# Block kernel (gated scan mixer, then routed experts): where TensorE waits as it enters the output and down projections

## The chip, the cores and the metric

The kernel runs on one core of one Trainium2 chip. The metric is the device time of one execution in microseconds. The kernel before took 505.88 us (median of three runs, 505.38 to 506.28).

## The reference

The input is 8 sequences of 1024 tokens with 256 features, in float32. What matters here:

```python
def mixer(x):                        # x normalised over its 256 features
    xp, z = split(x @ w_in)          # 512 channels each
    xc = silu(causal_conv(xp, 4 taps) + conv_b)
    h = h * 0.9 + 0.1 * (xc_t @ w_B) # 16 states, along the sequence
    return ((h @ w_C) * silu(z)) @ w_out
def experts(x):                      # x normalised again
    idx = top_k(x[:, 0, :] @ Wr + br, 2)      # by the first token of a sequence
    return mean over the 2 experts of gelu(x @ W1 + b1) @ W2 + b2
x = x + mixer(norm(x))
x = x + experts(norm(x))
```

## The kernel before

The 8192 tokens are cut into 16 chunks of 512. The work is a pipeline over chunks: step s runs the mixer's first part of chunk a = s, the output projection of chunk o = s - 1 and the experts of chunk f = s - 2. Each engine has its own program (`block.tensor`, `block.vector` and so on), written out by hand in order, and the programs meet at semaphores only. The first steps are an opening written out singly, steps 4 to 13 are a loop, and the last ones are written out again.

Every float32 product is made of three: an operand is split into a high and a low part, and TensorE computes high x high, high x low and low x high into the same accumulator. Two shapes of matmul fill its time. `project` (line 1290) makes 512-column products into a bank `blk` (six for a bank: first high and low weights with the high activations for both halves k, then the high weights with the low activations), and `state_in` (line 1466) makes eight 512-column ones into `turn`. `tokens` (line 1413) makes 256-column products into `tok`: here the activations are loaded as weights (`LDWEIGHTS`, 128 columns) and the weight matrix moves. One call of `tokens` makes two groups of three, lines 1419, 1420 and 1421. `out_proj` (line 1453) calls it four times for each of two halves h, 48 products in a row. `down` (line 1440) does the same, 24 products for h = 0 and 12 of h = 1, then comes `state_out` (line 1478, four 512-column products), then the other 12.

In `step` of TensorE (line 1571) the order is: the four `xp` projections, `out_proj` of both halves, the four `z` projections, the four `up` projections, `state_in`, `down` with `state_out` inside. So 256-column stretches start behind `xp` (the last `project`) or behind `state_in`, and in the last two steps behind `up`. At these 30 places `behind` (line 1424) stands ahead of the first product. It increments `paced`, a semaphore that nobody waits for, waits for a tail semaphore and increments `paced` three times more (`PACE`). The tail is incremented by the fourth-last matmul ahead: line 1297 in `project` (`x_tail`, `up_tail`) and line 1474 in `state_in` (`state_tail`). TensorE's instructions are handed out in order, so a wait holds all that stands behind it; a matmul call issues its weight load and its matmul.

Of the kernel before, what the change touches and what calls it, by code (L numbers as in the profile page):

```python
# [16 lines left out]
SQ = 32  # L17
QUADS = P // SQ
EARLY = 2
PACE = 3  # L20


def build_block(nc, x, w_in, conv_w, conv_b, w_B, w_C, w_out, Wr, br, W1, b1, W2, b2, out):
# [9 lines left out]
    KD = D // P  # L33
    JD = DI // P
    JF = TOP_K * KD
# [7 lines left out]
    with ExitStack() as ctx:  # L43
# [48 lines left out]
        w_out_hi, w_out_lo = sb("w_out_hi", [P, JD, D], F32R), sb("w_out_lo", [P, JD, D], F32R)  # L92
        w2_hi, w2_lo = sb("w2_hi", [P, TOP_K, KD * D], F32R), sb("w2_lo", [P, TOP_K, KD * D], F32R)
# [6 lines left out]
        y_hi, y_lo = sb("y_hi", [P, JD, CH], F32R), sb("y_lo", [P, JD, CH], F32R)  # L100
# [76 lines left out]
        paced = sem("paced")  # L177
# [1059 lines left out]
        def _(pe):  # L1237
            mm = nc.tensor.matmul
# [48 lines left out]
                    nc.tensor.transpose(blk[0][:, k * P:(k + 1) * P], by_token(normed2, 0)[:, k * P:(k + 1) * P],  # L1287
                                        ident[:]).then_inc(token_turned, 1)

            def project(bank, whi, wlo, his, los, ready, c, sem_out, fourth_last=None, between=None):  # L1290

                dst = bank[:]
                for k in range(KD):
                    if ready is not None:
                        pe.wait_ge(ready[0], c * KD + k + 1)
                    ins = mm(dst, whi(k), his(k), start=(k == 0), stop=False)  # L1296
                    if k == KD - 1 and fourth_last is not None:
                        ins.then_inc(fourth_last, 1)
                    mm(dst, wlo(k), his(k), start=False, stop=False)  # L1299
                    if k == 0 and between is not None:  # L1300
                        between()
                for k in range(KD):
                    if ready is not None:
                        pe.wait_ge(ready[1], c * KD + k + 1)
                    ins = mm(dst, whi(k), los(k), start=False, stop=(k == KD - 1))  # L1305
                ins.then_inc(sem_out, 1)

            def in_proj(a, j, part, bank, sem_out, between=None):
# [101 lines left out]
                            lambda k: w1_lo[:, 1, k * D + m * P:k * D + (m + 1) * P],  # L1410
                            lambda k: his[:, k, :], lambda k: los[:, k, :], None, 0, up_ready)

            def tokens(h, j, last, his, los, whi, wlo):


                for n in range(2):
                    rows = slice((2 * h + n) * P, (2 * h + n + 1) * P)
                    dst = tok[h][:, n * D:(n + 1) * D]
                    mm(dst, his[:, j, rows], whi, start=(j == 0 and n == 0), stop=False, skip_group_check=True)  # L1419
                    mm(dst, his[:, j, rows], wlo, start=False, stop=False, skip_group_check=True)  # L1420
                    ins = mm(dst, los[:, j, rows], whi, start=False, stop=(last and n == 1), skip_group_check=True)  # L1421
                return ins

            def behind(tail, count):
                pe.sem_inc(paced, 1)
                pe.wait_ge(tail, count)
                for _ in range(PACE):
                    pe.sem_inc(paced, 1)

            def down_tile(f, n, dst, js=range(JF)):  # L1430
                rows = slice(n * P, (n + 1) * P)
# [8 lines left out]
            def down(f, h, js=range(JF), tail=None):  # L1440
                for j in js:
                    if h == 0:
                        pe.wait_ge(g_lo, f * JF + j + 1)
                        if isinstance(f, int) and f == LAST - 1 and j % KD == 0:
                            pe.wait_ge(w2_lo_set, LAST // 2 * TOP_K + j // KD + 1)
                    if j == 0 and tail is not None:
                        behind(*tail)
                    t, cols = j // KD, slice(j % KD * D, (j % KD + 1) * D)
                    ins = tokens(h, j, j == JF - 1, hid_hi, hid_lo, w2_hi[:, t, cols], w2_lo[:, t, cols])
                if js[-1] == JF - 1:  # L1450
                    ins.then_inc(down_ready, 1)

            def out_proj(o, h, tail=None):
                pe.wait_ge(done, o * 2 + h + 1)
                for j in range(JD):
                    if h == 0:
                        if isinstance(o, int) and o == LAST and j:
                            pe.wait_ge(last_y_lo, j)
                        else:
                            pe.wait_ge(y_lo_set, o * JD + j + 1)  # L1460
                    if j == 0 and tail is not None:
                        behind(*tail)
                    ins = tokens(h, j, j == JD - 1, y_hi, y_lo, w_out_hi[:, j, :], w_out_lo[:, j, :])
                ins.then_inc(mixed, 1)

            def state_in(a):
                bank = u_bank(a)
                for j in range(JD):
                    pe.wait_ge(xc_hi_set, a * JD + j + 1)
                    mm(bank[:], b_mix[:, j, :], xc_hi[:, j, :], start=(j == 0), stop=False)  # L1470
                for j in range(JD):
                    pe.wait_ge(xc_lo_set, a * JD + JD if isinstance(a, int) and a < 3 else a * JD + j + 1)
                    ins = mm(bank[:], b_mix[:, j, :], xc_lo[:, j, :], start=False, stop=(j == JD - 1))  # L1473
                    if j == JD - 4:
                        ins.then_inc(state_tail, 1)
                ins.then_inc(u_ready, 1)

# [166 lines left out]
```

## Time and profile before

| | us |
|---|---|
| median of three runs | 505.88 (505.38 to 506.28) |
| the profiled execution, whole time | 507.02 |
| its span, first to last instruction | 505.1 |
| TensorE matmuls busy | 500.6 |
| TensorE weight loads busy | 442.7 |
| VectorE busy | 450.9 |
| ScalarE busy | 401.3 |
| GpSimd busy | 348.1 |

PE stands for TensorE's matmuls, PEld for its weight loads, PEldq for what its sequencer does itself. A matmul's duration is longer than the distance to the next start, since matmuls are pipelined; the distance between starts is what counts here.

### The profile page before, as it was taken

To read this page: it belongs to the slowest core of one execution; us is meant where nothing else is said; L and a number is where in the kernel's file an instruction comes from. 1 tells how busy PE (TensorE), PEld (TensorE's weight loads), DVE (VectorE), ACT (ScalarE), POOL (GpSimd) and SP (SyncE) were. 2 spreads that over 40 slices of the span, in tenths; PEclk is the share of its full clock that TensorE was granted. 3 is DMA by queue.
4 is the path that set the end of the run, shared out by engine and by line. 5 is a ranking of instruction groups with operands and counts; after the bars stand their busy time and mean duration, and the time that the engine had idled before them with its cause. 6 is when DMAs were issued, how large, how long until landed. Compare 5 with 4: busy or idle time off the path is not lost.

```text
span 505.1 us, 9943 instructions
## 1 busy us (share of the span) xinstructions
PE 500.6 (99%) x3026; PEld 442.7 (88%) x3026; DVE 450.9 (89%) x896; ACT 401.3 (79%) x692; POOL 348.1 (69%) x390
## 2 busy tenths in 40 slices
PE   8999999999999999999999999999999999999997
PEld 8888799888888988889888888988889889888997
DVE  6999999889998999989999899998999989996763
ACT  4986959888969788697987969878796888969454
POOL 4959597559693796929869197773977559673390
PEclk9999999999999999999999999999999999999999
DMA  8940105344250532605235170433614343130102
GB/s 254 300 180 7 37 1 183 110 135 160 77 191 27 166 125 86 204 30 193 68 126 165 48 227 16 166 125 100 191 42 150 99 132 120 59 108 1 42 3 84
DMA packets 53380, 57.29 MB, mean 113 GB/s; under 512 B 8682, under 2 KB 49642, under 8 KB 53226
## 3 DMA queue, kind: packets, MB, share of 16 engines
q1 hardware_dynamic: 51498, 56.67, 34.5%
q10 hardware_dynamic: 1856, 0.31, 0.3%
q8 instruction: 13, 0.21, 0.2%
q14 instruction: 13, 0.11, 0.1%
HBM read 35.46 MB, written 21.50 MB: 113 GB/s over the span
## 4 chain that ended last, share of the span: by engine, by line
PE 98%; DVE 1%; DMA 1%; issue 0%; DVEq 0%
PE blk L1296 16%; PE blk L1299 16%; PE blk L1305 16%; PE tok L1419 12%; PE tok L1420 12%; PE tok L1421 12%; PE blk L1494 3%; PE turn L1470 3%; PE turn L1473 3%; PE turn L1243 1%; PE tok L1299 1%; PE tok L1296 1%; PE tok L1305 1%; DMA x_mid<-in_L_attn_x 1%; DVE stats_t L917 0%; DVE normed L934 0%
## 5 line engine op out<-in xcount | busy, mean ns | idle before, releaser
L992 DVE SCALAR_TENSOR_TENSOR conv<-blk,tap_w,conv 128x512 f32<-128x512 f32 x192 | 130.1, 741 | 8.2 <-ACT conv L683 7.1
L488 POOL TENSOR_TENSOR y_lo<-gate,y_hi 128x512 fp32r<-128x512 f32 x57 | 72.2, 1297 | 35.5 <-ACT y_hi L611 35.4
L1296 PE MATMUL blk<-xn_hi,w_in_hi 128*128 128x512 f32 x228 | 89.4, 392 | 0.0
L1299 PE MATMUL blk<-xn_hi,w_in_lo 128*128 128x512 f32 x228 | 89.0, 391 | 0.0
L453 POOL TENSOR_TENSOR xc_lo<-conv,xc_hi 128x512 fp32r<-128x512 f32 x60 | 72.9, 1232 | 7.9 <-ACT xc_hi L611 7.7
L1419 PE MATMUL tok<-w_out_hi,y_hi 128*128 128x256 f32 x256 | 71.7, 280 | 0.0
L1420 PE MATMUL tok<-w_out_lo,y_hi 128*128 128x256 f32 x256 | 71.1, 278 | 0.0
L1421 PE MATMUL tok<-w_out_hi,y_lo 128*128 128x256 f32 x256 | 71.1, 278 | 0.0
L1305 PE MATMUL blk<-xn_lo,w_in_hi 128*128 128x512 f32 x228 | 70.3, 390 | 0.0
L1419 PE MATMUL tok<-w_hi,hid_hi 128*128 128x256 f32 x248 | 70.0, 282 | 0.0
L1421 PE MATMUL tok<-w_hi,hid_lo 128*128 128x256 f32 x248 | 69.6, 281 | 0.0
L1420 PE MATMUL tok<-w_lo,hid_hi 128*128 128x256 f32 x248 | 69.6, 281 | 0.0
L683 ACT ACTIVATE conv<-blk,tap_b,tap_w 128x512 f32<-128x512 f32 x64 | 49.3, 781 | 25.4 <-PE blk L1305 22.2
L689 ACT ACTIVATE conv<-conv 128x512 f32<-128x512 f32 x64 | 39.4, 632 | 30.3 <-DVE conv L992 29.4
L861 DVE TENSOR_TENSOR hid_lo<-hid,hid_hi 128x512 fp32r<-128x512 f32 x64 | 44.8, 728 | 17.1 <-ACT hid_hi L611 16.9
L498 POOL TENSOR_TENSOR x_mid<-x_mid,b_sel 128x256 f32<-128x256 f32 x60 | 45.7, 792 | 13.5 <-DVE hid_lo L861 9.4
L1305 PEld LDWEIGHTS blk<-xn_lo,w_in_hi 128*128 128x128 f32 x228 | 42.8, 188 | 9.1
L1419 PEld LDWEIGHTS tok<-w_out_hi,y_hi 128*128 128x128 f32 x256 | 48.3, 189 | 2.7 <-issue 2.6
L1299 PEld LDWEIGHTS blk<-xn_hi,w_in_lo 128*128 128x128 f32 x228 | 42.9, 188 | 8.1
L1419 PEld LDWEIGHTS tok<-w_hi,hid_hi 128*128 128x128 f32 x248 | 47.1, 190 | 3.1 <-issue 2.6
L1296 PEld LDWEIGHTS blk<-xn_hi,w_in_hi 128*128 128x128 f32 x228 | 42.8, 188 | 8.0
L1296 PE MATMUL blk<-xn_hi,w_hi 128*128 128x512 f32 x124 | 48.4, 390 | 0.0
(189 smaller groups left out, 1320.5 us busy)
## 6 DMA issues: line engine op xcount, KB each, us to landing
spill<-normed SPq DMA_DIRECT2D x25, 512.0 KB, 2.8
normed<-spill SPq DMA_DIRECT2D x100, 128.0 KB, 2.8
out<-x_mid SPq DMA_DIRECT2D x30, 256.0 KB, 2.5
x_mid<-in_L_attn_x SPq DMA_DIRECT2D x29, 256.0 KB, 2.7
x_in<-in_L_attn_x SPq DMA_DIRECT2D x14, 512.0 KB, 4.3
w_all<-in_L_ffn_W SPq DMA_DIRECT2D x2, 2048.0 KB, 11.4
b_all<-in_L_ffn_b SPq DMA_DIRECT2D x1, 1024.0 KB, 13.6
gate<-in_L_attn_w_in SPq DMA_DIRECT2D x2, 256.0 KB, 4.5
```

Source lines behind the costliest of these rows:

```text
L453: nc.gpsimd.tensor_tensor(xc_lo[:, j, :], conv[:, j, 0:CH], xc_hi[:, j, :].bitcast(F32), ALU.subtract).then_inc(xc_lo_set, 1)
L488: nc.gpsimd.tensor_tensor(y_lo[:, j, :], gate_of(o, j), y_hi[:, j, :].bitcast(F32), ALU.subtract).then_inc(y_lo_set, 1)
L498: ins = nc.gpsimd.tensor_tensor(mid(f, q)[:, n, :], mid(f, q)[:, n, :], b2_sel[:], ALU.add)
L683: nc.scalar.activation(conv[:, j, HALO:HALO + CH], blk[j][:], ACT.Identity, bias=tap_b[:, j:j + 1], scale=tap_w[:, j, 0:1]).then_inc(tap_f ...
L861: return nc.vector.tensor_tensor(dst, src, hi.bitcast(F32), ALU.subtract)
L992: nc.vector.scalar_tensor_tensor(cols, blk[j][:], tap_w[:, j, t:t + 1], cols, ALU.mult, ALU.add).then_inc(tap_added, 1)
L1296: ins = mm(dst, whi(k), his(k), start=(k == 0), stop=False)
L1299: mm(dst, wlo(k), his(k), start=False, stop=False)
L1305: ins = mm(dst, whi(k), los(k), start=False, stop=(k == KD - 1))
L1419: mm(dst, his[:, j, rows], whi, start=(j == 0 and n == 0), stop=False, skip_group_check=True)
L1420: mm(dst, his[:, j, rows], wlo, start=False, stop=False, skip_group_check=True)
L1421: ins = mm(dst, los[:, j, rows], whi, start=False, stop=(last and n == 1), skip_group_check=True)
```

## The change

The four semaphore operations of `behind` go. `tokens` takes the tail instead, and between its first and its second product TensorE waits for it and increments `paced` once. The tail is now incremented by the second-last matmul ahead, in `project` and in `state_in`. It is made at all 30 places. The arithmetic, its order and all buffers stay.

```diff
--- before.py
+++ after.py
@@ -17,7 +17,6 @@
 SQ = 32
 QUADS = P // SQ
 EARLY = 2
-PACE = 3
 
 
 def build_block(nc, x, w_in, conv_w, conv_b, w_B, w_C, w_out, Wr, br, W1, b1, W2, b2, out):
@@ -1287,15 +1286,13 @@
                     nc.tensor.transpose(blk[0][:, k * P:(k + 1) * P], by_token(normed2, 0)[:, k * P:(k + 1) * P],
                                         ident[:]).then_inc(token_turned, 1)
 
-            def project(bank, whi, wlo, his, los, ready, c, sem_out, fourth_last=None, between=None):
+            def project(bank, whi, wlo, his, los, ready, c, sem_out, tail=None, between=None):
 
                 dst = bank[:]
                 for k in range(KD):
                     if ready is not None:
                         pe.wait_ge(ready[0], c * KD + k + 1)
-                    ins = mm(dst, whi(k), his(k), start=(k == 0), stop=False)
-                    if k == KD - 1 and fourth_last is not None:
-                        ins.then_inc(fourth_last, 1)
+                    mm(dst, whi(k), his(k), start=(k == 0), stop=False)
                     mm(dst, wlo(k), his(k), start=False, stop=False)
                     if k == 0 and between is not None:
                         between()
@@ -1303,6 +1300,8 @@
                     if ready is not None:
                         pe.wait_ge(ready[1], c * KD + k + 1)
                     ins = mm(dst, whi(k), los(k), start=False, stop=(k == KD - 1))
+                    if k == KD - 2 and tail is not None:
+                        ins.then_inc(tail, 1)
                 ins.then_inc(sem_out, 1)
 
             def in_proj(a, j, part, bank, sem_out, between=None):
@@ -1410,22 +1409,19 @@
                             lambda k: w1_lo[:, 1, k * D + m * P:k * D + (m + 1) * P],
                             lambda k: his[:, k, :], lambda k: los[:, k, :], None, 0, up_ready)
 
-            def tokens(h, j, last, his, los, whi, wlo):
+            def tokens(h, j, last, his, los, whi, wlo, tail=None):
 
 
                 for n in range(2):
                     rows = slice((2 * h + n) * P, (2 * h + n + 1) * P)
                     dst = tok[h][:, n * D:(n + 1) * D]
                     mm(dst, his[:, j, rows], whi, start=(j == 0 and n == 0), stop=False, skip_group_check=True)
+                    if n == 0 and tail is not None:
+                        pe.wait_ge(*tail)
+                        pe.sem_inc(paced, 1)
                     mm(dst, his[:, j, rows], wlo, start=False, stop=False, skip_group_check=True)
                     ins = mm(dst, los[:, j, rows], whi, start=False, stop=(last and n == 1), skip_group_check=True)
                 return ins
-
-            def behind(tail, count):
-                pe.sem_inc(paced, 1)
-                pe.wait_ge(tail, count)
-                for _ in range(PACE):
-                    pe.sem_inc(paced, 1)
 
             def down_tile(f, n, dst, js=range(JF)):
                 rows = slice(n * P, (n + 1) * P)
@@ -1443,10 +1439,9 @@
                         pe.wait_ge(g_lo, f * JF + j + 1)
                         if isinstance(f, int) and f == LAST - 1 and j % KD == 0:
                             pe.wait_ge(w2_lo_set, LAST // 2 * TOP_K + j // KD + 1)
-                    if j == 0 and tail is not None:
-                        behind(*tail)
                     t, cols = j // KD, slice(j % KD * D, (j % KD + 1) * D)
-                    ins = tokens(h, j, j == JF - 1, hid_hi, hid_lo, w2_hi[:, t, cols], w2_lo[:, t, cols])
+                    ins = tokens(h, j, j == JF - 1, hid_hi, hid_lo, w2_hi[:, t, cols], w2_lo[:, t, cols],
+                                 tail if j == 0 else None)
                 if js[-1] == JF - 1:
                     ins.then_inc(down_ready, 1)
 
@@ -1458,9 +1453,8 @@
                             pe.wait_ge(last_y_lo, j)
                         else:
                             pe.wait_ge(y_lo_set, o * JD + j + 1)
-                    if j == 0 and tail is not None:
-                        behind(*tail)
-                    ins = tokens(h, j, j == JD - 1, y_hi, y_lo, w_out_hi[:, j, :], w_out_lo[:, j, :])
+                    ins = tokens(h, j, j == JD - 1, y_hi, y_lo, w_out_hi[:, j, :], w_out_lo[:, j, :],
+                                 tail if j == 0 else None)
                 ins.then_inc(mixed, 1)
 
             def state_in(a):
@@ -1471,7 +1465,7 @@
                 for j in range(JD):
                     pe.wait_ge(xc_lo_set, a * JD + JD if isinstance(a, int) and a < 3 else a * JD + j + 1)
                     ins = mm(bank[:], b_mix[:, j, :], xc_lo[:, j, :], start=False, stop=(j == JD - 1))
-                    if j == JD - 4:
+                    if j == JD - 2:
                         ins.then_inc(state_tail, 1)
                 ins.then_inc(u_ready, 1)
 
```

## Rows read from the trace of the kernel before

**Rows 1.** The page: engines, granted clock by slice, chain that ended last.

```profile
PE 500.6 (99%) x3026; PEld 442.7 (88%) x3026; DVE 450.9 (89%) x896; ACT 401.3 (79%) x692; POOL 348.1 (69%) x390
...
PEclk9999999999999999999999999999999999999999
...
PE 98%; DVE 1%; DMA 1%; issue 0%; DVEq 0%
```

**Rows 2.** Windows view, 256-column products into tok: window, us, busy (count), clock, DMA, GB/s.

```profile
41.04:46.68 5.64, 5.64 (x48) 1.00 0.01 3
63.98:72.19 8.21, 8.21 (x72) 1.00 0.01 2
82.29:87.95 5.66, 5.66 (x48) 1.00 0.62 177
100.67:104.80 4.13, 4.13 (x36) 1.00 0.04 6
112.84:118.56 5.72, 5.72 (x48) 1.00 0.74 230
143.33:148.80 5.47, 5.47 (x48) 1.00 0.56 189
192.01:196.33 4.32, 4.32 (x36) 1.00 0.30 121
252.80:257.05 4.25, 4.25 (x36) 1.00 0.30 123
257.98:259.39 1.41, 1.41 (x12) 1.00 0.43 130
264.86:270.36 5.50, 5.50 (x48) 1.00 0.53 179
416.84:422.50 5.66, 5.66 (x48) 1.00 0.48 172
```

**Rows 3.** Timeline around 252.80, matmuls, then weight loads: start us, us, engine, line, operation.

```profile
251.90 1.07 PE L1473 MATMUL turn<-xc_lo,b_mix 128*128 128x512 f32 x4
252.80 0.28 PE L1419 MATMUL tok<-w_hi,hid_hi 128*128 128x256 f32 x1
252.92 0.28 PE L1420 MATMUL tok<-w_lo,hid_hi 128*128 128x256 f32 x1
...
252.58 0.39 PE L1473 MATMUL turn<-xc_lo,b_mix 128*128 128x512 f32 x1
...
252.70 0.19 PEld L1419 LDWEIGHTS tok<-w_hi,hid_hi 128*128 128x128 f32 x1 [0.16 <-issue]
252.81 0.19 PEld L1420 LDWEIGHTS tok<-w_lo,hid_hi 128*128 128x128 f32 x1
```

**Rows 4.** Timeline around 143.33, matmuls, then weight loads.

```profile
143.33 0.29 PE L1419 MATMUL tok<-w_out_hi,y_hi 128*128 128x256 f32 x1
143.46 0.28 PE L1420 MATMUL tok<-w_out_lo,y_hi 128*128 128x256 f32 x1
...
143.23 0.19 PEld L1419 LDWEIGHTS tok<-w_out_hi,y_hi 128*128 128x128 f32 x1 [0.17 <-issue]
143.34 0.19 PEld L1420 LDWEIGHTS tok<-w_out_lo,y_hi 128*128 128x128 f32 x1
```

**Rows 5.** Timeline around 264.86, matmuls.

```profile
264.86 0.32 PE L1419 MATMUL tok<-w_out_hi,y_hi 128*128 128x256 f32 x1
265.01 0.29 PE L1420 MATMUL tok<-w_out_lo,y_hi 128*128 128x256 f32 x1
```

**Rows 6.** Timeline around 112.84, matmuls.

```profile
112.84 0.34 PE L1419 MATMUL tok<-w_out_hi,y_hi 128*128 128x256 f32 x1
113.02 0.28 PE L1420 MATMUL tok<-w_out_lo,y_hi 128*128 128x256 f32 x1
```

**Rows 7.** Line 1428 from 252.0 to 252.9: count, ns min/median/max, first and last start.

```profile
L1428 PEldq EVENT_SEMAPHORE  x3: 51/51/51, 252.3 to 252.6; - x3
```

## The prediction

> **What bounds the kernel now.** I read the page first [rows 1]: TensorE is busy for 500.6 of 505.1 us, the granted clock is full in all 40 slices, and the chain of waits that ended last is 98% TensorE. A wait on another engine hardly occurs, so a change to DVE, ACT, POOL or the DMA queues would be hidden, and this one touches none of them. Only the time from one matmul's start to the next one's start counts. So I went to the windows view, with each window laid on one unbroken stretch of the 256-column products into `tok` [rows 2], and divided its time by its count. Two steps come out, not one. The stretch at 82.29 needs 5.66/48 = 0.118 us per product, the one at 143.33 needs 5.47/48 = 0.114 us. The instructions are the same and the clock is 1.00 in both. I call them the long step (0.118) and the short step (0.113, once the first few products are off the mean). An interruption-free re-entry after `state_out` gives the long one (1.41/12 = 0.118), and does so each time.
>
> The 30 stretches that open with `behind` divide like this. Of the 14 of `out_proj` behind `x_tail`, nine run short (seven at 5.46 or 5.47, two at 5.50), four long (5.66, and one at 5.72), and the first (5.64) is long for its first half. The `out_proj` behind `state_tail` is short (8.21/72). Of the 15 of `down`, one is short (4.13), 13 long (4.24 or 4.25) and one long with a bad entry (4.32).
>
> Then I read the entries themselves, matmuls and weight loads side by side. At 252.80 [rows 3], a long one, the weights of the first product are loaded from 252.70, 0.10 before the product; undisturbed they would start with the matmul ahead, as those of the second product do (252.81 beside 252.80). At 143.33 [rows 4] the first two products stand 0.13 apart, in the short stretch. At 264.86 [rows 5] they stand 0.15 apart, short again; at 112.84 [rows 6] 0.18 apart, and that stretch is long. The entry thus costs between 0.00 and 0.06 us by itself, and it also decides which step the next 36 to 72 products take. The second is worth more: 48 x 0.0045 = 0.22 us.
>
> **The change, part by part.** (1) *Four semaphore instructions ahead of the first product go.* Three of them stand in a chain, 252.3 to 252.6 [rows 7], so 0.15 us from one to the next, and the first weight load follows 0.1 behind the last [rows 3]. Without them the first product's weights load behind the matmul ahead. That is worth what the first product was late: nothing visible at 252.80 (0.22 after the matmul at 252.58, like any 512-column one), 0.04 at 264.86 (0.32 long instead of 0.28), 0.06 at 112.84.
>
> (2) *The tail is now the second-last matmul instead of the fourth-last.* At 252.80 the fourth-last starts at 251.90 and the wait is over at 252.3, with the last of three instructions at 252.6 and the load at 252.70; counting back 0.08 + 2 x 0.15 puts the release at 252.33, that is 0.43 after the matmul's start. The second-last starts 0.45 later (252.35), so the new wait ends at 252.78.
>
> (3) *The wait stands between first and second product.* Everything behind it on TensorE's queue is held, the second product's weight load first. One load follows 0.08 after the last semaphore instruction, so this one starts at 252.86; now it starts at 252.81. From a load to its product 0.11 or 0.12 pass [rows 3], so the second product starts at 252.97 or 252.98: the first spacing becomes 0.165 to 0.175 where the long entries have 0.12. That is **+0.05 us per entry against the long ones**, about +0.04 against the 0.13 entries and +0.01 against the 0.155 ones. The bounds of the hold are 0.00 (if the load can start the moment the wait ends, 252.81) and 0.10. I take 0.05, since the load-to-semaphore distance is the same at every entry I read. Nobody else is late by it: DVE's `residual` and `finish` wait for the last product of the stretch. SP's and POOL's queues are not passed, no DMA moves, and the moved increment of `state_in` and `project` costs nothing, since it rides on a matmul as before. Each loop iteration computes its wait count on TensorE's sequencer; that is now done behind a first product, under four 512-column matmuls (0.9 us), and costs nothing as long as the sequencer is that far ahead.
>
> (4) *Which step follows.* No row of before shows this entry: the first product on time and its successor late. The entry is the same in all 30 places, and the fourth-last to load distance hardly varies, so I expect **one outcome for nearly all of them**. The nearest rows on either side disagree: first spacing 0.155 is short ([rows 5]; four entries look like that), 0.175 long ([rows 6]; one entry), 0.19 long (the 4.32 of [rows 2]). What speaks for short is that of the 13 entries whose first spacing is over 0.125, 11 run short, and that an undisturbed entry is always long, so leaving the long step wants a delay. I choose short, by little.
>
> The Trainium skill (TensorE: Matmul & The Clock Gate, section "Back-to-back issue gap") gives N/2.4 + 2.5 ns for warm matmuls, 109 ns at 256 columns; no stretch here reaches that, and the sum would be the same for both kernels by it.
>
> **The sum, if all run short.** `out_proj`: 48 x 0.1133 = 5.44, + 0.055 for the entry, + 0.02 to settle = 5.52, 14 times 77.3 against 77.6 now: -0.3. `down`: 36 x 0.1133 + 0.075 = 4.16, 15 times 62.4 against 63.6 now: -1.2. The 72-product stretch: +0.03. The last `down` runs on into its last tile with 12 products more: -0.05. Total -1.6 us (-0.3%). The profiled execution took 507.02 us with a span of 505.1, and so would be 505.4 after; the median of the runs, 505.88, lies 1.1 below it, and I give my number on that scale: **504.3 us**. Over the settling and the 0.00 to 0.10 of the hold (30 x 0.05 = 1.5 us each way at the extremes, half of that likely) this case spans 503.6 to 505.1.
>
> **Rivals.** *A: the new entry locks all stretches in the long step* (slower). It decides in the second and third product after the hold; it is the entry at 112.84 [rows 6], 0.18 apart, repeated 30 times. Then `out_proj` takes 48 x 0.1178 + 0.052 = 5.71, 14 times 79.9 (+2.3), `down` 4.29, 15 times 64.4 (+0.8), the 72-product stretch 8.53 (+0.3): +3.4, so 509.3 us. For it: the nearest single row, and that nine of 14 `out_proj` stretches have nothing to win. Against it: the 0.155 entries.
> *B: the two kinds split*, since `project` and `state_in` end differently, or a nanosecond decides: `out_proj` short and `down` long gives -0.3 + 0.8 + 0.1 = +0.6 (506.5), the reverse +2.3 - 1.2 = +1.1 (507.0); any mixture lies between 504.9 and 508.5.
> *C: the step is not set by the entry*, but by something that the change leaves alone, and the hold is a pure loss: 19 long entries x 0.05 + 11 short ones x 0.03 = +1.3, so 507.2 us. The trace speaks against it, since the same instructions run at both steps.
> By the Trainium skill (same page, "Step-by-step: what each phase is for") TensorE pulls weight loads ahead of matmuls in flight. The trace agrees in its 252.81 beside 252.80 [rows 3]; a semaphore wait between two products stops that, and by the rule alone the change would only lose, as in C.
> *D: the change doesn't hold anything*, since the tail is over before the sequencer gets there. Then all entries are like the one after `state_out`, all long: +1.9, 507.8 us. Against it: 252.78 is later than 252.35 by all of the sequencer's lead.
>
> **How the numbers follow.** Short everywhere 0.47, A 0.33, B 0.12, C 0.05, D 0.03. About 0.2% (1.0 us) is what a measurement of this kernel can tell from no change. The short case lies beyond that on the fast side for most of its span (0.43 of 0.47), with 0.02 more from B: faster 0.45. Within: 0.04 of the short case, 0.05 of B, 0.01 of C: 0.10. Slower: A, the rest of B, C and D: 0.45. Both signs hold much of the chance; the forecast's own range is 503.6 to 505.1, and to hold eight of ten the range must reach through A: 503.6 to 509.6.
>
> **What would show it.** Right: in the windows view the `out_proj` stretches take 5.50 to 5.54 and those of `down` 4.14 to 4.18; the first product's weight load starts with the last 512-column matmul, the second's 0.05 after the first product, and the products stand 0.16 to 0.175 apart; the chain of waits stays TensorE's at 98%. Step 3 is wrong if the first spacing stays at 0.12 or exceeds 0.20. Step 4 is wrong if the spacing is right and the stretches take 5.7 and 4.3. The forecast as a whole is wrong if any other engine appears in the chain with more than a per cent or two.

## The result, and the profile after

The changed kernel took **510.35 us** in the median of 4 runs (509.75 to 510.48), the kernel before 505.87 (505.38 to 506.28) beside it: ratio **1.0084**, 95% interval 1.0072 to 1.0095. The forecast was 504.3 us with a range of 503.6 to 509.6. It is missed in sign and just missed in range; the rival that came true is A, all entries in the long step. That is not the last word, though. In two later batches of runs, on two different chips, the same kernel came out 0.28% faster than before (e12) and level with it (e15, e16). The sections below show what differs between such executions; why it differs stays open.

The page of the changed kernel: busy time of the engines, the granted clock by slice, the chain that ended last.

```profile
PE 503.6 (99%) x3026; PEld 446.3 (88%) x3026; DVE 451.6 (89%) x896; ACT 400.4 (79%) x692; POOL 347.0 (68%) x390
...
PEclk9999999999999999999999999999999999999999
...
PE 98%; DVE 1%; DMA 1%; issue 0%; DVEq 0%
```

The same picture as [rows 1]: full clock, 98% of the chain on TensorE, the same 3026 matmuls. TensorE is busy 3.0 us longer, DVE, ACT and POOL within 1.1 us of before. What became longer is the stretches. The windows view of the changed kernel, one window on each unbroken stretch of 256-column products into `tok`; columns as in [rows 2] (window, us, busy and count, clock, DMA share, GB/s), and at the end the sum over all 31 such stretches:

```profile
41.17:46.92 5.75, 5.75 (x48) 1.00 0.01 3
64.20:72.73 8.53, 8.53 (x72) 1.00 0.01 2
82.82:88.52 5.70, 5.70 (x48) 1.00 0.55 163
144.40:150.10 5.70, 5.70 (x48) 1.00 0.54 184
254.84:259.12 4.28, 4.28 (x36) 1.00 0.30 123
420.22:425.92 5.70, 5.70 (x48) 1.00 0.48 177
...
sum 158.41, PE 158.38; mean PE 5.11
```

The stretch that was at 143.33 in [rows 2] and took 5.47 us takes 5.70; the one from 64.0 went from 8.21 to 8.53; the long `down` at 252.80 went from 4.25 to 4.28. None of the 30 stretches that open with the hold is short any more. (The 31st, from 476.89, has no hold in either kernel; it went from 5.81 to 5.72.) The same 31 windows of the kernel before add up to

```profile
sum 155.32, PE 155.29; mean PE 5.01
```

so 3.1 us of the 3.5 us between the two profiled executions (507.02 and 510.48) lie in these stretches.

One entry, the `down` at 254.84, in the timeline: matmuls first, then weight loads, as in [rows 3]; then the wait's own line, with its count, duration in ns and start.

```profile
253.94 1.07 PE L1467 MATMUL turn<-xc_lo,b_mix 128*128 128x512 f32 x4
254.84 0.28 PE L1418 MATMUL tok<-w_hi,hid_hi 128*128 128x256 f32 x1
254.96 0.33 PE L1422 MATMUL tok<-w_lo,hid_hi 128*128 128x256 f32 x1
255.12 0.28 PE L1423 MATMUL tok<-w_hi,hid_lo 128*128 128x256 f32 x1
...
254.62 0.19 PEld L1418 LDWEIGHTS tok<-w_hi,hid_hi 128*128 128x128 f32 x1
254.90 0.19 PEld L1422 LDWEIGHTS tok<-w_lo,hid_hi 128*128 128x128 f32 x1
...
L1421 PEldq EVENT_SEMAPHORE  x1: 51/51/51, 254.8 to 254.8; - x1
```

The first product's weights now load at 254.62, far ahead of it. The wait is over and its instruction runs at 254.8; the second product's load follows at 254.90, 0.06 behind the first product's start. The delay shows up one product later than I had put it: the second product starts on time (0.12 behind the first, and only 0.06 behind its own load) but is 0.33 long instead of 0.28, and the third starts 0.16 behind it.

### The profile page after: what moved, and what is told of

It is laid out like the page before. It is cut to its first block, busy times and chain, and to the rows that moved or that the text cites. A ratio compares the mean times of both kernels' runs of the same rounds, so it can differ in the third digit from the quotient of the medians.

```text
span 508.6 us, 9869 instructions
## 1 busy us (share of the span) xinstructions
PE 503.6 (99%) x3026; PEld 446.3 (88%) x3026; DVE 451.6 (89%) x896; ACT 400.4 (79%) x692; POOL 347.0 (68%) x390
## 4 chain that ended last, share of the span: by engine, by line
PE 98%; DVE 1%; DMA 1%; issue 0%; DVEq 0%
PE blk L1295 16%; PE blk L1296 16%; PE blk L1302 16%; PE tok L1422 12%; PE tok L1418 12%; PE tok L1423 12%; PE blk L1488 3%; PE turn L1464 3%; PE turn L1467 3%; PE turn L1242 1%; PE tok L1295 1%; PE tok L1296 1%; PE tok L1302 1%; DMA x_mid<-in_L_attn_x 1%; DVE stats_t L916 0%; DVE normed L933 0%
## 5 line engine op out<-in xcount | busy, mean ns | idle before, releaser
L1422 PE MATMUL tok<-w_out_lo,y_hi 128*128 128x256 f32 x256 | 72.5, 283 | 0.0
L1422 PEld LDWEIGHTS tok<-w_out_lo,y_hi 128*128 128x128 f32 x256 | 48.1, 188 | 1.4
L1422 PEld LDWEIGHTS tok<-w_lo,hid_hi 128*128 128x128 f32 x248 | 46.7, 188 | 1.9
```

## The experiments

Two theories after the result. **Theory:** the hold costs 0.05 us at each entry, 1.4 us in all, and the rest of the loss is the step that the entry leaves behind, decided by when the entry's weight load starts. **Rival:** a hold between two products always ends in the long step (or, in the later runs, the place in the program decides). Each batch of runs (e1 to e4, e5 to e7, e8 to e11, e12 to e14, e15 to e17) had its own runs of the kernel before beside it and went to a chip of its own, of the same kind; which chip the first comparison ran on is not recorded.

An entry is called short or long here by the products right behind it. In the first stretch (from 41 us) that is not the whole stretch: around its 19th product one or two starts are 0.14 to 0.23 us apart, and behind that gap the step can be the other one, from long to short in before and in e1, from short to long in e14 and e16.

**e1, the wait and its increment removed** (the kernel before's four instructions are gone too; what order the wait enforced is a matter of pace alone):

```diff
-                    if n == 0 and tail is not None:
-                        pe.wait_ge(*tail)
-                        pe.sem_inc(paced, 1)
```

> The changed kernel without its wait and its increment: nothing stands between the first and the second product, nothing ahead of the first. Theory (the entry sets the step; the hold itself costs 0.045 us): every one of the 30 stretches enters as the ones after state_out do and runs at the long step, 5.66 for 48 products and 4.24 for 36, so 30 x 0.045 = 1.35 us less than the changed kernel: 509.0 us, and still 3 us slower than before, which then is the price of losing before's 11 short stretches. Rival (the hold between two products is what makes the step long): short stretches appear, 5.44 and 4.08 us, and the time falls below 505. Rival (the hold is nearly all of the loss): 506 to 507 us.

Measured: 508.93 us, ratio to before 1.0061 [1.0044, 1.0078]. All 30 entries long, without the delay:

```profile
82.62:88.27 5.65, 5.65 (x48) 1.00 0.56 167
100.99:105.23 4.24, 4.24 (x36) 1.00 0.04 6
```

Against the change's 5.70 and 4.28 that is 0.05 us per entry; over the 31 stretches 158.41 against 156.98, 1.4 us. The hold is 1.4 us of the loss, and an entry that nothing delays is long. The theory's 509.0 us came true. This kernel is also what the prediction's rival D describes (nothing held, all long, +1.9 us): its stretches are 1.7 us longer than those of before (156.98 against 155.32), and so is its profiled execution (508.69 against 507.02).

**e2, one more increment in the hold:**

```diff
                         pe.wait_ge(*tail)
-                        pe.sem_inc(paced, 1)
+                        for _ in range(2):
+                            pe.sem_inc(paced, 1)
```

> The changed kernel with one more increment of the unused semaphore in the hold, so that the second product's weights load 0.15 us later than in the changed kernel (0.2 behind the first product). Theory (when the second product starts sets the step, not that something is held): the entry costs 0.195 instead of 0.045 us, 30 x 0.15 = 4.5 us more; if this entry leads to the short step too, 30 stretches win 0.16 to 0.22 each, 5.4 us back, so 509.5; if it leads to the long step 514.9. Rival (any hold between two products gives the long step): 514.9 us with 5.85 and 4.43 us in the windows.

Measured: 509.62 us, 1.0072 [1.0055, 1.0089]. All 30 entries short. The entry of the `down` at 253.96 in the timeline, matmuls, then the second product's load:

```profile
253.96 0.28 PE L1418 MATMUL tok<-w_hi,hid_hi 128*128 128x256 f32 x1
254.20 0.36 PE L1423 MATMUL tok<-w_lo,hid_hi 128*128 128x256 f32 x1
254.39 0.28 PE L1424 MATMUL tok<-w_hi,hid_lo 128*128 128x256 f32 x1
254.51 0.28 PE L1418 MATMUL tok<-w_hi,hid_hi 128*128 128x256 f32 x1
254.62 0.28 PE L1423 MATMUL tok<-w_lo,hid_hi 128*128 128x256 f32 x1
254.74 0.28 PE L1424 MATMUL tok<-w_hi,hid_lo 128*128 128x256 f32 x1
...
254.17 0.19 PEld L1423 LDWEIGHTS tok<-w_lo,hid_hi 128*128 128x128 f32 x1 [0.24 <-issue]
```

The second product is 0.24 behind the first and the third 0.19, which is 0.2 us of delay, four times that of the change, and yet `out_proj` takes 5.66 and `down` 4.29: from there on the products stand 0.113 to 0.116 apart. The longer hold is not dearer than the change with all its entries long; it is dearer than the change with short ones, as e12 and e13 show on one chip. "A hold always gives the long step" falls.

**e3, the tail moved to the third-last matmul, three increments in the hold:**

```diff
-                    if j == JD - 2:
+                    if j == JD - 3:
                         ins.then_inc(state_tail, 1)
```

(the same in `project`, and `range(3)` in the hold)

> The hold at the changed kernel's place, but on the third-last matmul and with three increments: the wait ends 0.23 earlier and the chain takes 0.30 longer, so the second product's weights load 0.13 behind the first product instead of 0.056. The entry costs 0.12. Theory: 30 x 0.07 = 2.2 us more than the changed kernel if it leads to the long step (512.6), and 5.4 less than that if it leads to the short one (507.2). Rival (any hold between two products gives the long step): 512.6.

Measured: 509.52 us, 1.0076 [1.0057, 1.0094]; 29 of 30 entries short, as the theory has it, but above its number. The load came 0.13 to 0.17 behind the first product, and the 31 stretches of the profiled execution (508.19 us) are 156.38 us, 1 us more than the estimate had room for; the median lies another 1.3 us above that execution, unexplained. Step right, size wrong.

**e4, the hold back ahead of the first product, on the third-last matmul, one increment and a register move:**

```diff
+                    if n == 0 and tail is not None:
+                        pe.wait_ge(*tail)
+                        pe.sem_inc(paced, 1)
+                        pe.reg_mov(spare, 1)
                     mm(dst, his[:, j, rows], whi, start=(j == 0 and n == 0), stop=False, skip_group_check=True)
```

> No hold between products: the wait stands ahead of the first product, as in the kernel before, but on the third-last matmul, with one increment and one register move in place of before's three increments. The first weight load then comes 0.06 to 0.08 ahead of the first product (before: 0.10). Before's entries at 0.07 all ran short. Theory: all or nearly all of the 30 stretches run short, 5.49 for 48 products and 4.12 for 36: 14 x 5.49 + 15 x 4.12 = 138.7 against 141.2 us before, 503.4 us. Rival (which step follows doesn't hang on the entry's lead): as many short and long ones as before, 505.9, or as the changed kernel 509 to 510.

Measured: 507.70 us, 1.0035 [1.0023, 1.0048]: a miss. The trace has no instruction for the register move, so the compiler had dropped it and the load was not as late as intended. The run became useful by accident. At 15 entries the compiler had put the waits into two semaphore instructions, at 15 into one. Two `down`s and an `out_proj` in the windows view, and the timeline (matmuls, loads) of the first:

```profile
162.02:166.16 4.14, 4.14 (x36) 1.00 0.04 6
192.59:196.83 4.24, 4.24 (x36) 1.00 0.30 124
143.65:149.30 5.65, 5.65 (x48) 1.00 0.59 181
...
162.02 0.33 PE L1423 MATMUL tok<-w_hi,hid_hi 128*128 128x256 f32 x1
162.19 0.28 PE L1424 MATMUL tok<-w_lo,hid_hi 128*128 128x256 f32 x1
...
161.96 0.19 PEld L1423 LDWEIGHTS tok<-w_hi,hid_hi 128*128 128x128 f32 x1 [0.20 <-issue]
```

With two instructions the load starts 0.06 ahead of its product, where undisturbed it starts 0.2 ahead; the next product is 0.17 behind; all 15 entries of this kind are short. With one instruction the load is hardly late (the `out_proj` at 143.65 loads at 143.47), and all 15 are long. Same kernel, same execution, both outcomes, and here the lateness of the load sorts them (e9, e10 and e14 below show that it does not do so everywhere).

**e5, two instructions at every entry.** Waits that are long satisfied are put ahead of the tail's, so that the tail's gets an instruction of its own in the loops as well (the edit at `out_proj`; `down` has the like):

```diff
+                        for passed_by in tail[2:]:
+                            pe.wait_ge(*passed_by)
+                        pe.wait_ge(*tail[:2])
...
-                    out_proj(o, 0, (x_tail, a + 1) if has_attn(s) else None)
+                    out_proj(o, 0, (x_tail, a + 1, *(() if isinstance(s, int) else ((done, a + 1), (consts_set, 3)))) if has_attn(s) else None)
```

> The wait stands ahead of the first product again, on TensorE's third-last matmul in front, and at all 30 entries in two semaphore instructions: one that waits for the tail alone, one that carries the other waits and the increment (in the loops an already satisfied wait is added so that there are two). e4 had this form at about half of its entries; each of those entered with the first weight load 0.065 us ahead of the first product, had a first spacing of 0.165 us and then the short step, while those with one instruction had the load in time and the long step. Theory (when the entry's load starts sets the step): all 30 entries come out short, out_proj 5.51 us, down 4.15, the 72 products 8.23, together 153.4 us against 155.3 in the profiled execution of before; the other work of the span took 351.7 to 352.1 us in each profile so far, so 505.3 us, within 0.3% of before's median and 5 us under the change. Rival (the step hangs on which place of the program it is: the loops' out_proj and every other down were long in e4 because of where they stand): they stay long, 5.75 and 4.29 us with the added delay, and the time is 508.5 us or more.

Measured: 505.90 us, before 506.17, ratio 0.9998 [0.9988, 1.0007]; 29 of 30 short (5.50 and 4.14), the sum 153.59. The places that were long in e4 are short here, so the place is not what decides. Against before's profiled execution the stretches are 1.7 us shorter and the time is 1.1 us less; against before's median on this chip, where before was not profiled, nothing is left of it.

**e6 and e7, the change at one kind of entry, before's hold at the other** (a condition on the semaphore at the tail, the hold and `behind`):

```diff
-                    if n == 0 and tail is not None:
+                    if n == 0 and tail is not None and tail[0] is x_tail:
```

> The change at the 14 output projections that wait behind an input projection alone; the other 16 entries keep before's fourth-last matmul and hold in front. Theory (the change costs its hold and the loss of the short step, entry by entry): the 14 take 5.70 us each (79.8 us against 77.6 in the profiled execution of before), the others as before (77.7 us), together 157.5 against 155.3: about 508.1 us by the median of before, up to 509.4 by its profiled execution. Rival (the entries are coupled: a change at one kind moves the alignment of the next): the down projections, untouched here, change their step too, in either direction, and the time is outside 507.5 to 509.5 us.

> The counterpart: the change at the down projections and the one output projection behind the state product, 16 entries; the 14 output projections keep before's tail and hold. Theory: the 16 go from 77.7 to 78.5 us, nearly all hold, the 14 output projections stay at 77.6 us or less with most of them short: about 507.0 us by the median of before, 508.0 by its profiled execution; with the run before it the two costs add up to the whole 4.5 us of the change. Rival (coupled): the 14 untouched output projections all turn long (5.66 us), and the time is 508.5 to 509.5 us.

Measured: 507.92 us, 1.0043 [1.0029, 1.0057], and 507.67 us, 1.0038 [1.0024, 1.0052]. The changed entries are all long in both (5.70; 4.29). The untouched ones are not as before, an `out_proj` and a `down` of e6, then of e7:

```profile
235.18:240.88 5.70, 5.70 (x48) 1.00 0.75 237
253.60:257.71 4.11, 4.11 (x36) 1.00 0.31 128
...
235.17:240.64 5.47, 5.47 (x48) 1.00 0.63 197
253.36:257.65 4.29, 4.29 (x36) 1.00 0.30 122
```

In e6 15 of the 16 untouched entries are short, of which 2 were before; in e7 all 14 are, of which 9 were. The coupled rival is right that untouched entries move, wrong about the direction in e7 and about the time in both (it wanted one outside 507.5 to 509.5 us for e6, and 508.5 to 509.5 for e7). The theory's 508.1 us for e6 fits the 507.92, but not for its reason, since the untouched entries did not stay as they were. The costs of the two halves, 1.75 and 1.5 us, do not add up to the whole.

**e8, the kernel before once more**, nothing changed.

> The kernel before itself, profiled once more and timed against itself. Theory (with a load lead of about 0.10 us an entry's step is decided afresh in each execution): the profile shows another set of short and long entries than the 11 short ones of the first profile, and its time follows the count: 351.8 us and the sum of the 31 stretches. Rival (the place in the program decides): the same 11 entries are short again. The ratio is 1 in either case, its interval some 0.1% wide.

Measured: 507.50 us beside 507.31, 1.0003 [0.9994, 1.0012]; the same kernel is 1.4 us slower here than in the first comparison. 14 entries are short, and 7 of the 30 changed sides, so neither the kernel nor the place in it fixes an entry's step; three that changed (compare 63.98, 143.33 and 192.01 in [rows 2]):

```profile
63.87:72.36 8.49, 8.49 (x72) 1.00 0.01 2
143.83:149.56 5.73, 5.73 (x48) 1.00 0.55 183
192.75:196.87 4.12, 4.12 (x36) 1.00 0.31 126
```

**e9 and e10, the form of e5 at one kind, before's at the other** (edit as in e6, on the kernel of e5).

> The 14 output projections behind an input projection keep before's fourth-last matmul and hold in front (load lead 0.10 us, first spacing 0.12); the other 16 entries take the form of e5 (third-last matmul, two waits, lead 0.065 us, first spacing 0.165). Theory (what a lead of 0.065 us gives is certain, what a lead of 0.10 gives hangs on how the work in front arrived): the 16 are short (76.3 us), and the output projections are short as well when they were in e7, 5.47 us each: 152.9 us in all and 504.7 us. Rival (e7's short output projections were chance): they are mixed again, up to 5.66 us each, and the time is 505.5 to 507.3 us, no better than before.

> The counterpart: the 14 output projections in the form of e5 (5.50 us each), the other 16 entries in before's form. Theory: the down projections are short at 4.11 us as 12 of 15 were in e6, 152.7 us in all and 504.5 us. Rival: they are long as 14 of 15 were in the first profile of before (4.25 us), 154.7 us in all and 506.5 us.

Measured: 508.13 us, 1.0015 [1.0006, 1.0024], with 8 entries short, and 508.64 us, 1.0026 [1.0015, 1.0036], with 11. Both theories fall: the form that was short 29 times of 30 in e5 is short at 7 of 16 entries in e9 and 8 of 14 in e10. A load 0.06 ahead of its product is no guarantee.

**e11, the change's second-last matmul with the wait ahead of the first product:**

```diff
+                    if n == 0 and tail is not None:
+                        pe.wait_ge(*tail)
+                        pe.sem_inc(paced, 1)
                     mm(dst, his[:, j, rows], whi, start=(j == 0 and n == 0), stop=False, skip_group_check=True)
```

> The change's tail, the second-last matmul, but the wait ahead of the first product as before, with one increment. From the durations so far (wait over 0.43 us after the tail's start, 0.08 us from a single semaphore instruction to the weight load, 0.11 more for a second one, 0.11 from load to product) the first product of an entry is 0.17 to 0.27 us late, against 0.05 for the second product in the change. Theory: an entry costs 0.2 us, all long 163 us and 515 us, all short 158 us and 510 us; short if a load later than its slot gives the short step as in e2 and e3. Rival (the place of the wait is of no matter, since the products run behind the sequencer's front): the time is that of the change, 510.3 us, with long steps.

Measured: 512.92 us, 1.0110 [1.0095, 1.0126], in the middle of the theory's 510 to 515; 12 of 30 short. A `down` in the timeline: matmuls, and the first product's load.

```profile
254.38 1.07 PE L1467 MATMUL turn<-xc_lo,b_mix 128*128 128x512 f32 x4
255.32 0.36 PE L1421 MATMUL tok<-w_hi,hid_hi 128*128 128x256 f32 x1
...
255.29 0.19 PEld L1421 LDWEIGHTS tok<-w_hi,hid_hi 128*128 128x128 f32 x1 [0.27 <-issue]
```

The first product's load is only 0.03 ahead of it, and the product starts 0.94 behind the first of the four 512-column matmuls where it is 0.90 in the change. This entry is one of the least late; others start up to 0.24 us late. Over the kernel the time less the 31 stretches (157.03) is 355.6 us, 3.7 above what the other kernels show (table below): 0.12 us per entry are lost ahead of the first product, and its own spacing of 0.19 comes on top. Behind the first product the same wait costs 0.05 (e1). The rival, that the place of the wait is of no matter, falls.

**e12, e13, e14: the change, e2 and e5 once more, on one chip.**

> The changed kernel once more, with a second profile. Theory (the second product's load 0.056 us after the first product gives the long step whatever the execution): again all 30 entries long, out_proj 5.70 and down 4.29 us, the 31 stretches 158.4 us, 510.2 us, and a narrower scatter than the kernel before. Rival (the outcome was that of one execution): some entries are short, each 0.23 or 0.15 us less; with a third of them short 508.3 us.

> The kernel of e2 once more: one more increment in the hold, nothing else changed against the run before. Theory: again all 30 entries short (31 stretches 157.9 us) and 509.6 us, 0.5 us under the change in spite of 0.07 us more delay at each entry. Rival (chance): mixed, each long one adding 0.2 us; with half of them long 512.5 us.

> The kernel of e5 once more. If its 29 short entries hung on that one call, some entries come out long here with a first spacing of 0.157 us, as in e9 and e10: with half of them long 508.5 us and 1 to 2 us above before. If e9 and e10 were mixed because two forms alternate in them, all are short again, 505.4 to 505.9 us.

Measured: **506.15 us for the change against 507.43 for before, ratio 0.9972 [0.9960, 0.9983]**; 509.46 us for e2's kernel, 1.0041 [1.0027, 1.0056]; 508.52 us for e5's, 1.0023 [1.0013, 1.0032]. Seven of the change's nine executions lie at 505.53 to 506.27; the profiled one is the highest (509.82), with 10 entries short. The theory that the change's entry is long whatever the execution falls. e2's kernel is short at all 30 again, as expected, but on this chip it is 3.3 us slower than the change, where 0.5 us faster had been expected. e5's kernel is short at 10, so the 29 of e5 were one draw, and one form alone is as uneven here as the two forms of e9 and e10. The change, last of the three in the batches before, is first here.

**e15, e16, e17: the change twice more, and e1 again, on one chip.**

> The changed kernel a third time. Theory (each execution's time is 351.8 us and the sum of its 31 stretches; the hold of 0.05 us at an entry can end in either step, differently from chip to chip): an execution of 506 us shows some 24 or more of the 30 entries short, out_proj 5.51 and down 4.15 us, one of 510 us all long. Rival (what was saved lies elsewhere): a profiled execution near 506 us shows mostly long entries and shorter work between them.

> The same kernel once more, for a second profile on the same chip: on one chip most executions agree (within 0.8 us in the first call and in 7 of 9 of e12), so this profile's count of short entries is near that of the run before it. Rival (a draw at each execution, whatever the chip): the two profiles and the times spread over 506 to 510 us alike.

> The kernel of e1 once more, no wait and no increment. Theory (an entry that nothing delays keeps the long step): again all 30 long, 508.8 us on whatever chip. Rival (the free run varies by chip like the change does): some short, each 0.2 us less, down to 504 us with all short.

Measured: 506.86 and 506.77 us beside 506.82, ratios 0.9998 [0.9989, 1.0007] and 0.9997 [0.9988, 1.0006]; 508.61 us without hold, 1.0037 [1.0024, 1.0051], all 30 long. e15's profile has 22 entries short, e16's all 30, so two executions on one chip differ too; e16's profiled execution (505.94) is the second-fastest of its 11. Without hold the theory's 508.8 us and all entries long came true. An `out_proj` and a `down` of e16 and its sum:

```profile
234.76:240.27 5.51, 5.51 (x48) 1.00 0.67 222
252.99:257.14 4.15, 4.15 (x36) 1.00 0.31 126
...
sum 154.07, PE 153.81; mean PE 4.96
```

The same instructions took 5.70 and 4.28 in the first profile. The two entries differ by nanoseconds; the second product's line in the first profile of the change (long), then in e16 (short), duration in ns as min/median/max:

```profile
L1422 PE MATMUL tok<-w_lo,hid_hi x1: 326/326/326, 255.0 to 255.0; 128*128 128x256 f32 x1
```

```profile
L1422 PE MATMUL tok<-w_lo,hid_hi x1: 323/323/323, 253.1 to 253.1; 128*128 128x256 f32 x1
```

In the four profiles of the change (120 entries) this record sorts all of them: it is 317 to 324 ns in the 62 short entries and 326 or 327 in the 58 long ones. The outcome is thus already visible at the second product. What makes it 323 or 326 is not shown.

**One sum over all profiles.** Short entries, the sum of the 31 stretches, the time of the profiled execution, and what remains, in us:

| kernel | short of 30 | 31 stretches | time | rest |
|---|---|---|---|---|
| before | 11 | 155.32 | 507.02 | 351.7 |
| before, e8 | 14 | 155.08 | 507.50 | 352.4 |
| change | 0 | 158.41 | 510.48 | 352.1 |
| change, e12 | 10 | 156.87 | 509.82 | 353.0 |
| change, e15 | 22 | 154.98 | 506.92 | 351.9 |
| change, e16 | 30 | 154.07 | 505.94 | 351.9 |
| no hold, e1 / e17 | 0 / 0 | 156.98 / 156.90 | 508.69 / 508.55 | 351.7 / 351.7 |
| longer hold, e2 / e13 | 30 / 30 | 157.86 / 157.65 | 509.65 / 509.39 | 351.8 / 351.7 |
| e5's form, e5 / e14 | 29 / 10 | 153.59 / 156.61 | 505.89 / 508.65 | 352.3 / 352.0 |
| e3 / e4 | 29 / 15 | 156.38 / 155.35 | 508.19 / 507.47 | 351.8 / 352.1 |
| e6 / e7 | 15 / 14 | 155.82 / 155.73 | 507.52 / 507.69 | 351.7 / 352.0 |
| e9 / e10 | 8 / 11 | 156.64 / 155.96 | 508.51 / 508.59 | 351.9 / 352.6 |
| wait in front, e11 | 12 | 157.03 | 512.63 | 355.6 |

The rest is 351.7 to 352.6 us in all but two: in e12 the first stretch begins at 42.09, about 1 us later than elsewhere, and e11 loses time ahead of its entries. Up to that 1 us, what separates the other kernels, and the executions of one kernel, is the stretches.

## Why the prediction was wrong

**What bounds the kernel** was right: TensorE, and in it the spacing of the 256-column products, as the table shows. The chain that ended last is TensorE's at 92% or more in every profile. My own sign of being wrong, another engine with more than a per cent or two in it, did show: DVE has 3 or 4% in e7, e8, e10 and e16. Their rest in the table is 351.9 to 352.6 us, so any cost of it is well under 1 us.

**Step 1**, the four instructions removed are worth almost nothing. Right: without any wait the long entries go from 4.25 [rows 2] to 4.24 (e1).

**Step 2**, the new wait ends 0.43 after the second-last matmul's start. Right: that matmul starts at 254.39 (253.94 and two times 0.227), the semaphore instruction runs at 254.8. The distance is 0.43 at all 30 places of the first profile.

**Step 3**, the hold costs 0.05 us per entry. Right in size: the load came 0.06 behind the first product, and the change and e1 differ by 1.4 us over 30 entries, 0.048 each. Wrong in place: I expected the first spacing to be 0.165 to 0.175; it stayed 0.12 and the second became 0.16. The term that failed is the 0.11 or 0.12 from a load to its product: the held load stands only 0.06 ahead of its product.

**Step 4, "Which step follows", is the one that failed.** It held three claims. That the entry goes with the step and the step carries most of the money: right, and rival A's windows (5.71, 4.29, 8.53) are what the first profile shows (5.70, 4.28, 8.53). That there would be one outcome for nearly all: right for the first profile (30 long) and for e16 (30 short), wrong for e12 (10 short) and e15 (22). And the choice of short: wrong in the comparison that counts. I chose it from the first spacing in five rows of before, as if 0.155 and 0.175 were two sides of a threshold. The runs show that there is none to be read there: first spacings near 0.155 went both ways. One of 0.155 was short in before [rows 5], 0.157 long in e14 and 0.160 short in e14 again, and the change's own second spacing, about 0.163 in the long entries and 0.160 in the short ones, splits on some 3 ns. e8 shows the same of before: 7 of 30 entries changed sides between two profiles. Nor is the re-entry behind `state_out` long each time, as it was in before: in the change's first profile one of them ran short (from 137.43, 12 products in 1.37 us), its first product 0.235 us behind the matmul ahead instead of 0.229. When the outcome turned out short, the forecast's numbers came true: 5.51 and 4.15 in e16 where it had 5.50 to 5.54 and 4.14 to 4.18, and 505.94 us for a profiled execution where it had 505.4.

Two outcomes with nearly even chances was the honest reading, and the chances given said so (0.47 and 0.33). What the text did not have is that the same kernel could take either from one batch or execution to the next, so that no single comparison is the kernel's. Beside e12's -1.3 us the forecast's -1.6 would have looked right, beside e15 and e16 (0.0) it would have missed with the change level: which of them came first was luck.

Two slips in the sum cancel: the 15 `down` stretches of before add up to 63.7 us, not 63.6, so that term is -1.3; with the -1.2 as written the terms add up to -1.5, not -1.6. And rival B's mixtures can lie anywhere between all short (504.3) and A (509.3), not only from 504.9 to 508.5.

**The range** ended at 509.6 because A's +3.4 was set on the median, 505.88. On the scale of the profiled executions A gives 507.02 + 3.4 = 510.4 us, and 510.48 was measured. Before's profiled execution lay 1.1 us above its own median, and I treated that offset as one that the changed kernel would share. It is no constant: the changed kernel had hardly any in the first comparison (510.48 against 510.35), and before had none in e8 (507.50 in both). That more entries ran short in the other executions of before would explain it, but none of those was profiled.

The Trainium skill (TensorE: Matmul & The Clock Gate, "Back-to-back issue gap") gives one spacing for a warm 256-column matmul by itself, 109 ns, and says that in a stream both the weight load and the matmul set it. No stretch of this case reaches the 109. For the second part the traces show only that the same stream of loads and matmuls runs at 113 or 118 ns, full clock in both, and that it keeps its spacing for up to 72 products where nothing interrupts it.

**What stays open.** Why there are two steps, what sets the few nanoseconds that go with one or the other, and what a chip contributes. Each batch ran on another chip at another time, so the two are not told apart. The granted clock is 1.00 in both steps, and DMA traffic does not sort them: its share is 0.75 in a long `out_proj` of e6 and 0.67 in a short one of e16. That the 505.5 to 506.3 us executions of e12 were all short is argued from the sum, not seen; e16 at 505.94 is the profile that shows such an execution. No version beat the kernel before in two batches: the change was slower, faster and level, e5's form level in one and 0.23% slower in another.

## What to carry to other kernels

When the trace shows the same instructions at two rates, count how many stretches run at each in more than one profile before forecasting anything below their difference: one profile is one draw. An edit can be robust, with the same outcome in both of its profiles (no hold: all long; the longer hold: all short), and still be no gain: both were slower than before each time, by 0.37 to 0.72%. A comparison on one chip with a narrow interval says little of such a draw in the next batch. And set a forecast on the scale of the execution whose rows were summed, unless it is known why that execution and the median differ.

## What the runs showed that I had not expected

- A delay can pay for itself. 0.2 us of hold (e2, 157.86 us for the stretches) cost no more than 0.05 us in the first profile of the change (158.41), because all its entries were short in both profiles. Against the change with all entries short (e16, 154.07) it costs 3.8 us.
- A kernel's ratio to another changed sign between batches: 1.0084, 0.9972 and 0.9998, each with an interval of about 0.1% on either side. The kernel before itself had medians from 505.87 to 507.50 us.
- Semaphore instructions on TensorE's queue did not all cost the same: in e4 the one that only waits was followed by the next after 0.1 us (161.8 and 161.9), while three with increments stand 0.15 apart [rows 7].
